# First cross attention: V's last chunk behind K's second tile and in another PSUM bank, the turned rows in its old one

## Time and profile before

| what | value |
|---|---|
| device time, median of 3 runs | 1944.19 us (1941.96 to 1944.48) |
| device time of the profiled execution | 1942.46 us |
| its span, first to last instruction | 1940.6 us |
| PE busy | 1862.6 us, 96% |
| DVE busy | 1501.2 us, 77% |
| ACT busy | 1271.0 us, 65% |
| POOL busy | 950.7 us, 49% |
| mean granted TensorE clock | 0.981 of full speed |

### The profile page before, as it was taken

How to read it: one execution, slowest core, us unless ns; L and a number is a source line. 1 busy time by engine, 2 the same in 40 slices (tenths; PEclk the granted TensorE clock), 3 DMA queues, 4 the chain that set the end, 5 groups by cost and what they waited for, 6 DMA issues and landing times.

```text
span 1940.6 us, 61563 instructions
## 1 busy us (share of the span) xinstructions
PE 1862.6 (96%) x20887; PEld 1636.0 (84%) x20887; DVE 1501.2 (77%) x3438; ACT 1271.0 (65%) x2720; POOL 950.7 (49%) x1616
## 2 busy tenths in 40 slices
PE   6999999999899999889999999969999999999996
PEld 5888888888678888679999999958888888988885
DVE  6777887878478878756666666657999999998986
ACT  2555555555477777557777777747777777777773
POOL 4556655665256667630000000057676767677751
PEclk9999999999899999889999999979999999999998
DMA  8222233222051111265555555421111111111100
GB/s 239 91 89 89 89 106 101 89 89 64 11 178 31 38 38 37 61 242 197 203 194 189 197 203 194 162 82 57 37 37 39 33 42 30 42 32 41 34 16 10
DMA packets 116595, 182.05 MB, mean 94 GB/s; under 512 B 10850, under 2 KB 94562, under 8 KB 116066
## 3 DMA queue, kind: packets, MB, share of 16 engines
q1 hardware_dynamic: 110386, 166.51, 26.8%
q0 software_dynamic: 6144, 14.69, 2.6%
HBM read 127.68 MB, written 53.48 MB: 93 GB/s over the span
## 4 chain that ended last, share of the span: by engine, by line
PE 54%; DVE 2%; DMA 1%; POOL 1%; issue 1%; ACT 0%; SPq 0%; ACTq 0%; DVEq 0%; POOLq 0%
PE ps_quad L1518 11%; PE ps_out L1538 9%; PE ps_quad L182 6%; PE ps_turned L108 4%; PE ps_quad L102 4%; PE ps_out L114 4%; PE ps_proj L1989 3%; PE ps_turned L182 3%; PE ps_quad L1969 3%; PE ps_proj L182 2%; PE ps_proj L1994 1%; PE ps_proj L1526 1%; DMA c_wv<-in_L_xattn_Wv 0%; PE ps_quad L1984 0%; PE ps_proj L1984 0%
## 5 line engine op out<-in xcount | busy, mean ns | idle before, releaser
L1518 PE MATMUL ps_quad<-e_xT,w 128*128 128x128 f32 x2016 | 235.3, 275 | 1.8 <-DVE e_xT L1476 1.8
L1518 PEld LDWEIGHTS ps_quad<-e_xT,w 128*128 128x128 f32 x2016 | 230.4, 192 | 2.2 <-DVE e_xT L1476 2.2
L369 ACT ACTIVATE a_probsT<-ps_quad 125x1792 f32<-125x1792 f32 x96 | 159.9, 1666 | 98.2 <-PE ps_quad L549 98.2
L1658 POOL TENSOR_TENSOR c_held<-minus_half 1x1 f32<-1x1 f32 x32 | 9.6, 302 | 409.8 <-DMA slots<-e_y 407.3
L1433 ACT ACTIVATE e_act_T<-ps_quad,fc_b 128x128 f32<-128x128 f32 x504 | 136.8, 383 | 91.7 <-PE ps_quad L1518 91.5
L126 DVE TENSOR_SCALAR c_probs<-c_probs,c_recip 112x375 f32<-112x375 f32 x256 | 163.2, 678 | 4.6
L134 ACT ACTIVATE c_probs<-ps_quad,c_negmax 112x375 f32<-112x375 f32 x256 | 143.6, 570 | 32.8 <-DVE c_negmax L119 32.8
L1538 PE MATMUL ps_out<-e_w2H,e_aH 128*128 128x256 f32 x504 | 149.0, 296 | 7.6 <-DVE e_w2L L1464 7.5
L1464 DVE TENSOR_TENSOR e_w2L<-w,e_w2H 128x1024 fp32r<-128x1024 f32 x126 | 150.4, 1235 | 0.0
L119 DVE TENSOR_REDUCE c_negmax<-ps_quad 112x2 f32<-112x750 f32 x128 | 113.9, 930 | 42.4 <-PE ps_quad L102 42.4
L434 DVE TENSOR_REDUCE a_negmax<-ps_turned 112x2 f32<-112x750 f32 x128 | 120.1, 939 | 34.0 <-PE ps_turned L535 33.8
(11 more groups left out here) (356 smaller groups left out, 6008.9 us busy)
## 6 DMA issues: line engine op xcount, KB each, us to landing
w<-in_fc_t SPq DMA_DIRECT2D x71, 1024.0 KB, 4.9
slots<-a_zeros SPq DMA_DIRECT2D x60, 512.0 KB, 4.9
a_cT<-in_ctx_t SPq DMA_DIRECT2D x32, 375.0 KB, 3.5
c_cT<-in_ctx_t SPq DMA_DIRECT2D x32, 375.0 KB, 3.2
e_xg<-slots SPq DMA_DIRECT2D x63, 128.0 KB, 3.9
slots<-e_y SPq DMA_DIRECT2D x63, 128.0 KB, 1.8
out<-c_fo SPq DMA_DIRECT2D x32, 112.0 KB, 1.9
residual<-in_x SPq DMA_DIRECT2D x1, 2912.0 KB, 19.3
```

What stands on the lines that cost most here:

```text
L369: act.activation(probsT[:, 2 * i:2 * i + 2, :, :].rearrange("p c r x -> p r c x"), quad[0:KC, :, 0:2 * HALF].rearrange("p r (c x) -> p r c ...
L1518: last = pe.matmul(hidden[par][:, c // 4, (c % 4) * TILE:(c % 4 + 1) * TILE], mem["w1"][:, par, k, c * 128:(c + 1) * 128], xT[par][:, k, : ...
```

## The change

In `step` of PE, v_product(2) moves from behind the turned rows (6 above) to directly behind k_product(1) (2 above), and goes to `plain[0:KC, 1, 0:D]` in place of `proj[0:KC, 0:D]`. Before it PE waits for the fifth maximum, since that one reads `plain`. The turned rows (5) go to `proj[:, 0:HALF]` in place of `plain[:, 1, 0:HALF]`, and the wait for k_whole, ACT's copy of K's second tile, now stands before them. ACT's copy of xT and DVE's copy of V's last chunk read the new places. No instruction is added or taken away but for waits.

```diff
-                        act.activation(xT[...], plain[:, 1, 0:HALF], ACT.Copy).then_inc(xT_ready, 1)
+                        act.activation(xT[...], proj[:, 0:HALF], ACT.Copy).then_inc(xT_ready, 1)
...
-                    dve.tensor_tensor(v[to][:, 2, :, 0:HD], proj[0:KC, 0:D]...
+                    dve.tensor_tensor(v[to][:, 2, :, 0:HD], plain[0:KC, 1, 0:D]...
...
-                        to = proj[0:KC, D:2 * D] if c == 1 else proj[0:KC, 0:D]
+                        to = (proj[0:KC, 0:D], proj[0:KC, D:2 * D], plain[0:KC, 1, 0:D])[c]
...
                     if exists(later):
                         pe.wait_ge(k_whole, 2 * later + 1)
                         k_product(1)
+                        if exists(nxt):
+                            pe.wait_ge(max_ready, 6 * nxt + 5)
+                        if isinstance(b, int) and later == 0:
+                            pe.wait_ge(w_split, 2)
+                        v_product(2).then_inc(v_mm, 1)
...
                         pe.wait_ge(norm.rows_ready, later + 1)
                         if isinstance(b, int) and later == 0:
                             pe.wait_ge(weights_in, 32)
-                            pe.wait_ge(w_split, 2)
+                        pe.wait_ge(k_whole, 2 * later + 2)
                         for k in range(2):
-                            last = pe.transpose(plain[:, 1, k * T:(k + 1) * T], xn[:, k * 128:(k + 1) * 128], ident[0:T, 0:T])
+                            last = pe.transpose(proj[:, k * T:(k + 1) * T], xn[:, k * 128:(k + 1) * 128], ident[0:T, 0:T])
                         last.then_inc(xT_mm, 1)
-                        pe.wait_ge(k_whole, 2 * later + 2)
-                        v_product(2).then_inc(v_mm, 1)
                     if exists(nxt):
                         pe.wait_ge(max_ready, 6 * nxt + 6)
                         pe.wait_ge(shift_ready, 2 * nxt + 1)
                         shift_turn(1)
```

More of the change, by code:

```diff
@@ L397, in step @@
                         wait(act, q_mm, later)
-                        act.activation(xT[:, :, :].rearrange("p k t -> p (k t)"), plain[:, 1, 0:HALF], ACT.Copy).then_inc(xT_ready, 1)
+                        act.activation(xT[:, :, :].rearrange("p k t -> p (k t)"), proj[:, 0:HALF], ACT.Copy).then_inc(xT_ready, 1)
                     if isinstance(b, int) and b == NB - 1:
@@ L441, in v_copy_last @@
                     wait(dve, values_ready, 2 * (b - 1))
-                    dve.tensor_tensor(v[to][:, 2, :, 0:HD], proj[0:KC, 0:D].rearrange("p (h d) -> p h d", h=H),
+                    dve.tensor_tensor(v[to][:, 2, :, 0:HD], plain[0:KC, 1, 0:D].rearrange("p (h d) -> p h d", h=H),
                                       bv[0:KC, :].rearrange("p (h d) -> p h d", h=H), ALU.add).then_inc(v_ready, 1)
```

## The result

The changed kernel takes 1953.74 us (median of 6 runs, 1951.67 to 1959.21), the kernel before on the same chip 1944.10 us (6 runs, 1941.96 to 1946.18): 9.6 us more, a ratio of 1.0055 with an interval of 1.0044 to 1.0067. It is slower, as forecast; of the 12.2 us forecast, 9.6 came.

The account below looks back on a forecast made before the run. PE was taken as the bound, in a ring with ACT's exponentials, its solo stretch without slack. Batches +12.5 and stage ends -0.3 gave +12.2 us on 1944.19, so 1956.4 us, range 1951 to 1961 us.

Parts of the forecast that it names:

- V behind K, without wait or open load: V's start in each batch: no wait for K's copy, load hidden under K's last matmul; 4.2 us gain by itself.
- The cover is gone: Between the shift turns sharing a bank, V no longer hides ACT's copy; net +0.38 or +0.45 us per batch, 12.5 in all.
- Forecast marks: Signs expected in the profile after: shift copy at 1.61, second turn's load at 2.09, a new PE wait of 0.3 to 0.4 us.
- Rival A: Faster: K and V have different banks and nothing else gets late; 1939.3 us, 6% chance.
- Rival B: No difference: PE's load waits elsewhere in the ring swallow the 0.4 us per batch; 1944 us stays, 11% chance.
- Rival C: Dearer: V's load stays open and the scaled rows come late by 0.1; 6 us more, 1962.4 us, 9% chance.
- PE's answer: Delay from the end of ACT's first shift copy to the second turn's load; taken as 0.12 us, lower end 0.05.
- later kind: Batches where ACT starts K's copy 0.28 us after the transposes; 15 assumed, each +0.38 us.
- earlier kind: Batches where ACT starts K's copy 0.20 us after the transposes; 15 assumed, each +0.45 us.
- The open load of the second turn: Second shift turn's weight load not hidden behind other work; 0.05 us per batch, 1.5 us in all.
- The start of the stage: Steps -2 and -1: a gain of 0.74 us and a loss of 0.41 us, together -0.3 us.

Follow-up runs that it names:

- v_behind_shift: Changed kernel with V's last chunk moved behind the first shift turn, ahead of the turned rows; 1938.36 us, 0.9976 of the kernel before.
- row_turns_thrice: Changed kernel with the pair of turned rows done three times, as filling ahead of the second shift turn; 1952.50 us, 1.0036 of the kernel before.
- shift_in_pieces: Changed kernel with ACT copying the first shift turn in four pieces of 56 columns; 1960.70 us, 1.0074 of the kernel before.
- before_in_pieces: Kernel before the change with ACT copying the first shift turn in four pieces of 56 columns; 1945.79 us, ratio 1.0007.
- shift_two_banks: Changed kernel with the first shift turn in a bank of the quad scores, so the second needn't wait for its copy; 1953.45 us, ratio 1.0046.
- one_wait_each: Changed kernel with the sixth-maximum wait moved ahead of the row turn, leaving the second shift turn only the copy's wait; 1954.75 us, ratio 1.0050.
- banks_alone: Changed kernel with V's last chunk back behind the turned rows, leaving only the bank swap and the moved K-copy wait; 1951.21 us, ratio 1.0044.
- both_paths: Changed kernel with V's last chunk behind the oT transposes and the first shift turn in a quad scores bank; 1938.92 us, ratio 0.9965.

## Why the prediction was right, and where it was off

- **V behind K, without wait or open load.** As forecast: 0.17 behind K's last matmul, every batch. Most of the 4.2 us of gain is real: the batches of v_behind_shift are 0.128 shorter than before, 3.8 us for 30.
- **The cover is gone.** As forecast, and shown from both sides: filling ahead of the second turn costs nothing (row_turns_thrice), a longer copy costs its own length (shift_in_pieces), the same copy under V's cover nearly nothing (before_in_pieces), and V put back as a cover wins it all (v_behind_shift). Forecast marks behind K's last matmul: ACT's copy 1.61, measured 1.59 (400.55, 402.14, and 416.11, 417.70); the second load 2.09, measured 2.06 and 2.00; PE's wait 0.3 to 0.4, measured 0.31.
- **Rival A** (faster) fell on the condition it was given: the copy would have to be back by the end of the row turn, but starts only there (417.70 against 417.50 + 0.19). The Trainium skill (Perfetto Trace Analysis, section Matmuls) advises rotating independent groups through banks. V and K do so here, with a gain where the copy stays covered (v_behind_shift); the two shift turns don't, and with V out from between them their shared bank is what PE waits for.
- **Rival B** (slack) fell: 0.36 of the 0.41 forecast for each batch reached the period.
- **Rival C**: V's load was hidden, and the scaled rows weren't last. They were only 0.06 from it (shift_two_banks); the forecast had them "nearly as long".
- **The term that was mis-sized: PE's answer.** I took 0.12 for all 30 batches, from the query product's row with two waits. Measured: 0.05 in 13 batches, 0.11 in 16. The 13 are the batches of the later kind of the earlier trace rows, so those were over-forecast (scores 0.29 later than before in place of 0.38), and those of the earlier kind hardly (0.42 in place of 0.45). I had also counted 15 of each kind; the trace before has 13 and 17, which is worth 0.1 us. V's start to the scores is so 2.36 or 2.43 where the steps of the forecast add up to 2.46. The mean, (13 x 2.36 + 16 x 2.43) / 29 = 2.40, is 0.06 less, and 30 x 0.06 = 1.8 us. The period says the same: 0.364 for 0.415, 1.5 us.
- **The open load of the second turn**, 0.05, was there: the `on` turn follows 0.25 behind (418.36 - 418.11), 0.19 where the load is hidden (420.70 - 420.51 in v_behind_shift). By the Trainium skill (TensorE: Matmul & The Clock Gate, section Step-by-step: what each phase is for) the engine pulls loads ahead of matmuls in flight; the trace shows that this load, which has its own semaphore to wait for, starts only when that has come.
- **The start of the stage.** Forecast a gain of 0.3. The query product came at 14.55 (forecast 14.65, before 15.39), and the scores of step -1 at 31.93 (before 32.37): 0.84 gained, 0.40 of it lost again, as forecast. But K's second tile of step 0 is at 43.98 in place of 44.74, so 0.3 more were won on the way there. The trace places them at the first plain scores of step -1: in the kernel before these wait for DVE's copy of q and start 1.29 behind the second group of scores (36.66 and 35.37), in the changed kernel 0.98 behind it (35.91 and 34.93), and the rest of the way is the same. Why DVE is earlier there I didn't test. The two executions also differ in the clock: between 20 and 31 us it was 0.50 in the profile after and 1.00 in that of before, so the start is compared less safely than the batches, where it is 1.00 in both.
- **The sum.** 10.56 for the 29 batches, 0.36 for the last, 0.76 off at the start: +10.2, where 9.6 was measured. The forecast's +12.2 was too high by the 1.5 of the answer and the 0.45 at the start; the remaining 0.6 is within the spread of the medians. The profiled execution itself took 1959.21, 5.5 above its own median and 4.5 above the 1954.7 forecast for it. From K's second tile of step 29 to the end it takes 1464.9 us, against 1457.9 in the profile before, 7.0 more, of which the last batch's delay is 0.4. Most of the rest goes with a lower granted clock there (below), so I don't count it to the change.

## What to carry to other kernels

When work is moved up because its own wait can be taken away, ask what it was covering where it stood: here five matmuls hid an ACT copy between two uses of one bank, and the place behind the first of these uses kept both the gain and the cover. A second chain of nearly the same length hides such a cause from single edits; try the edits in pairs before calling either worthless. To see whether an engine stands still at a place, put harmless work there: if the period stays, it does.

## What the runs showed that I hadn't expected

**Two waits, two answers.** The same instruction with two waits answers the copy 0.05 us after its end in 13 batches and 0.11 after it in 16; with one wait it is 0.05 in all 29. The 0.11 stands in every batch in which ACT's copy of K ends early, 1.74 behind K's start, and the 0.05 in every one in which it ends at 1.82. These kinds alternate, so it goes with the half of the unrolled loop; one_wait_each has both kinds and 0.05 in all. Two more rows fit: V in the kernel before, with one wait, answers in 0.05 in all 30 batches, and the row turn of banks_alone, with two, in 0.11 in all. Why the second wait costs nothing in one half of the loop is open.

**The clock at the end of the stage.** Windows of 12 us that begin 16 us after K's second tile of step 29, after, v_behind_shift and before_in_pieces (columns as in the first window):

```profile
508.54:520.54 12.00, 10.49 (x120) 8.05 (x121) 3.98 (x18) 5.76 (x8) 2.15 (x6) 0.72 0.00 1
```

```profile
493.94:505.94 12.00, 9.98 (x196) 8.23 (x200) 3.47 (x18) 7.73 (x13) 2.15 (x6) 1.00 0.00 1
```

```profile
500.38:512.38 12.00, 10.90 (x162) 8.43 (x166) 3.58 (x18) 7.31 (x12) 2.16 (x6) 0.86 0.00 1
```

There the stretches of PE alone end. In the changed kernel PE was busy 3.4 of the 5 us in which the clock began to fall (505 to 510), and from 510 to 516 us the granted clock was 0.50, the 1.2 GHz level:

```profile
505.00:510.00 5.00, 3.41 (x66) 2.21 (x62) 4.73 (x7) 0.90 (x2) 0.36 (x1) 0.95 0.02 3
510.00:513.00 3.00, 3.00 (x36) 2.42 (x36) 0.58 (x5) 0.86 (x3) 1.42 (x5) 0.50 0.00 0
```

The idle time alone doesn't decide it: the kernel before was busy 3.2 of 5 us at the same distance behind that tile (495.2 to 500.2) and kept 1.00. Over the 12 us the granted clock was 1.00 in before and v_behind_shift, 0.86 in six of the others and 0.72 in three. From K's second tile of step 29 to the last output product it took 32.1 and 32.0 us in the two with 1.00, 34.5 in the three with 0.72 (after: 492.54 to 527.02). The 34.5 hold 0.3 to 0.4 us of delay of batch 29 itself, so about 2 us of a profiled execution can come from the clock there. More comes later: from 320 to 400 us behind that tile it was 0.81 in the profile after (812.54 to 892.54) and 0.85 in that of before (802.74 to 882.74), worth 3 us if PE's work takes twice as long at the lower level (an estimate). Kernels with the same work show it and don't (v_behind_shift and both_paths, with nearly the same batch, 1.00 and 0.86), so I put it down to the execution and not to the change. Whether the change makes it more likely stays open: one profile of each kernel can't tell.
